# Second block's context attention: one VectorE pass per query chunk takes the maximum over both key halves, for two of four heads

## The reference, cut to what matters

```python
q = jnp.einsum('bsc,hcd->bhsd', xn, wq)
k = jnp.einsum('btc,hcd->bhtd', yn, wk)
v = jnp.einsum('btc,hcd->bhtd', yn, wv)
a = jax.nn.softmax(jnp.einsum('bhsd,bhtd->bhst', q, k) * D ** (-0.5), axis=-1)
o = jnp.einsum('bhst,bhtd->bhsd', a, v)
```

## Time and profile before

| | |
|---|---|
| median of 3 runs | 1450.94 us |
| lowest, highest | 1449.52, 1451.96 us |
| profiled execution, first to last instruction (span) | 1480.6 us |
| profiled execution, own time beside the span | not given |
| mean granted TensorE clock | 0.975 of 2.4 GHz |
| busy: TensorE, VectorE, ScalarE, GpSimd | 1407.8, 837.4, 762.4, 576.4 us |

### The profile page before, as it was taken

How to read it: one execution, slowest core, us unless ns; L and a number is a source line. 1 busy time by engine, 2 the same in 40 slices (tenths; PEclk the granted TensorE clock), 3 DMA queues, 4 the chain that set the end, 5 groups by cost and what they waited for, 6 DMA issues and landing times.

```text
span 1480.6 us, 24805 instructions
## 1 busy us (share of the span) xinstructions
PE 1407.8 (95%) x9880; PEld 807.5 (55%) x9880; DVE 837.4 (57%) x1739; ACT 762.4 (51%) x1161; POOL 576.4 (39%) x629
## 2 busy tenths in 40 slices
PE   8999999999999988899999999998999999997997
PEld 5677853333333256787653433753344445667996
DVE  3288547669999464126763774346788882222221
ACT  4544225656666645233254777332688885323331
POOL 3053134233334333521021565501688886405111
PEclk9999999999999999899999999997799999998999
DMA  7000000000110048562300002404000001833100
GB/s 226 1 1 1 1 12 1 15 8 16 44 40 19 3 152 297 195 220 68 33 23 0 10 24 79 130 0 135 1 10 16 9 16 38 330 118 102 34 17 10
DMA packets 81810, 90.85 MB, mean 61 GB/s; under 512 B 31969, under 2 KB 65726, under 8 KB 80543
## 3 DMA queue, kind: packets, MB, share of 16 engines
q1 hardware_dynamic: 78782, 83.01, 18.2%
q0 software_dynamic: 2912, 6.26, 1.2%
HBM read 67.92 MB, written 21.48 MB: 60 GB/s over the span
## 4 chain that ended last, share of the span: by engine, by line
PE 85%; DVE 9%; issue 2%; ACT 2%; POOL 1%; another core or an unknown queue 1%; DMA 0%; POOLq 0%; DVEq 0%; ACTq 0%
PE psum L1717 12%; PE psum L1736 10%; PE psum L1675 6%; PE psum L4140 6%; PE psum L736 4%; PE psum L3392 4%; PE psum L3383 4%; PE psum L1933 4%; PE psum L1759 3%; PE psum L4151 3%; PE psum L2863 2%; DVE a_nm L1846 2%; PE psum L2869 2%; PE psum L3361 2%; PE psum L724 2%
## 5 line engine op out<-in xcount | busy, mean ns | idle before, releaser
L1846 DVE TENSOR_REDUCE a_nm<-psum 128x1 f32<-128x512 f32 x302 | 199.6, 686 | 99.8 <-PE psum L1675 97.3
L1846 DVE TENSOR_REDUCE xa_nm<-psum 128x1 f32<-128x512 f32 x256 | 161.8, 683 | 49.6 <-PE psum L1675 44.0
L1771 ACT ACTIVATE xn<-psum 128x1024 f32<-128x1024 f32 (+1 forms) x96 | 86.2, 949 | 52.0 <-PE psum L1717 52.0
L1771 ACT ACTIVATE a_w<-psum 128x1024 f32<-128x1024 f32 x86 | 83.4, 1021 | 17.8 <-PE psum L1717 17.3
L1717 PE MATMUL psum<-a2qT,a2kT 32*128 32x512 f32 x512 | 90.3, 608 | 0.0
L1771 ACT ACTIVATE xa_w<-psum 128x1024 f32<-128x1024 f32 (+2 forms) x96 | 79.7, 885 | 19.6 <-PE psum L1717 19.4
L1675 PE MATMUL psum<-a2kr,a2qr 32*128 32x512 bf16 x256 | 71.5, 408 | 6.4 <-DVE a_nm L1846 5.7
L1707 PE MATMUL psum<-a_mrow,onesb 2*128 2x512 bf16 x384 | 69.2, 392 | 0.3 <-DVE a_mrow L1875 0.2
L1675 PE MATMUL psum<-xa_ckr,xa_cqr 32*128 32x512 bf16 x256 | 65.7, 382 | 1.7 <-POOL xa_ckr L1980 1.0
L1675 PEld LDWEIGHTS psum<-a2kr,a2qr 32*128 32x128 bf16 x256 | 20.8, 92 | 76.0 <-DVE a_nm L1846 49.2
L670 POOL TENSOR_SCALAR pf_kdd<-pf_kdd 128x1024 f32<-128x1024 f32 x8 | 22.2, 2775 | 97.2 <-ACT pf_kdd L841 97.2
(11 more groups left out here) (591 smaller groups left out, 3488.4 us busy)
## 6 DMA issues: line engine op xcount, KB each, us to landing
mo_w<-in_L_ffn_W SPq DMA_DIRECT2D x14, 1024.0 KB
sw_wv<-in_L_ffn_w_v SPq DMA_DIRECT2D x4, 2048.0 KB, 18.9
scratch_a2v<-co_stages SPq DMA_DIRECT2D x16, 256.0 KB
scratch_a2k<-co_stages SPq DMA_DIRECT2D x16, 256.0 KB
a2kT<-scratch_a2k SPq DMA_DIRECT2D x8, 512.0 KB, 7.8
a2v<-scratch_a2v SPq DMA_DIRECT2D x4, 1024.0 KB, 11.7
sw_wp<-in_L_ffn_w_proj SPq DMA_DIRECT2D x4, 1024.0 KB, 19.6
a_raw<-scratch_a_dens SPq DMA_DIRECT2D x56, 64.0 KB, 2.1
```

The source lines that it names most:

```text
L1771: e.activation(self.weights(n, c)[:, 2 * jj:2 * jj + 2, lo:S], ps[:, pr:pr + 2, lo:S], ACT.Exp, scale=self.scale).then_inc(*self.weighed.m ...
L1846: e.tensor_reduce(self.nm[n % 3][:, q, part, h:h + 1], view, AX.X, ALU.max, negate=True).then_inc(*self.max_taken.mark(*i))
```

## The change

Keys of heads 2 and 3 in the first half are replaced, in the rounded keys only, by the difference of first and second half. A maximum item of such a head and half ("excess") is then q(k1 - k2), the amount by which the first score exceeds the second. ScalarE copies it with a rectifier instead of plainly. The item of the second half ("lower") is then handled by one VectorE instruction, `tensor_tensor_reduce`: second half plus rectified difference, which is the larger of the two scores, with the sign turned and the minimum over the row as a second output. So heads 2 and 3 have one VectorE pass for two items, heads 0 and 1 two passes as before. The columns of `nm` that no pass writes are set to 1e30 once, by GpSimd. The order of the items changes to [excess, lower, plain, plain], where the lower one belongs to the excess item of the four before; the differences are kept also in the lead-in (in two tiles that are free there), where they are no longer VectorE's. In the planner the kept item no longer has its own VectorE pass right behind the second maximum. GpSimd's rounding becomes three instructions a group. The first attention of the block (`a1`) goes on as before. Not shown: the constructor's and `keep_maxima`'s new arguments, the memset, and the wait on it.

```diff
     def place(self, step):
+        if self.a.is_excess(step[1]):
+            yield from self.keep(step)
+            return
...
-        self.take(step, self.now + time, self.TAKE)
+        self.take(step, max(self.now + time, self.outstanding.pop(step[1], 0.0)), self.TAKE)
...
-        self.held = step[1], self.scalar
+        if self.a.paired:
+            self.outstanding[self.a.taker(step[1])] = self.scalar
+        else:
+            self.held = step[1], self.scalar
...
     def pair_kept(self, n):
 
-        if self.fits(n, "rows"):
+        if self.a.paired:
+            step = self.among(n, self.a.is_excess) or self.among(n, self.is_upper)
+            if step:
+                yield from self.place(step)
+        elif self.fits(n, "rows"):
             yield from self.keep(self.chosen((2, 3)))
 
+    def among(self, n, kind):
+
+        return next((step for step in self.maxima_left()[:4] if kind(step[1])), None) if self.fits(n, "rows") else None
+
+    def is_upper(self, item):
+        return item[3] > 1 and (item in self.outstanding if self.a.is_lower(item) else not self.a.is_excess(item))
+
     def behind_rows(self, n, c):
-        if self.held and self.fits(n, "rows"):
+        if self.a.paired:
+            step = self.among(n, self.is_upper)
+            if step:
+                yield from self.place(step)
+        elif self.held and self.fits(n, "rows"):
             yield from self.place(self.chosen((2, 3)))
         yield from self.held_taken()
 
     def pair_behind(self, n):
         for count in range(2):
-            if self.fits(n, "rows"):
+            if self.a.paired:
+                step = self.among(n, lambda item: item[3] < 2)
+                if step:
+                    yield from self.place(step)
+            elif self.fits(n, "rows"):
                 yield from self.place(self.chosen((0, 1)))
...
+    def paired_items(self, n, t):
+
+        i, half = divmod(t, 2)
+        excess, plain = [(n, i, 0, 2 + half)], [(n, i, half, 0), (n, i, half, 1)]
+        lower = [(n, i, 1, 2) if half else (n, i - 1, 1, 3)]
+        return (excess if t < 2 * SC else []) + (lower if t else []) + (plain if t < 2 * SC else [])
...
-            yield step
+            if step[0] == "max" and self.is_excess(step[1]):
+                self.keep_next(step[1])
+                yield "keep", step[1]
+            else:
+                yield step
...
-                e.activation(kept[:, :], ps[:, self.pair_of("max", *i), :], ACT.Copy).then_inc(*self.max_kept.mark(*i))
+                e.activation(kept[:, :], ps[:, self.pair_of("max", *i), :], ACT.Relu if self.paired else ACT.Copy).then_inc(*self.max_kept.mark(*i))
...
+                elif self.is_lower(i):
+                    w.wait_ge(*self.max_kept.at(*self.excess_of(i)))
+                    kept, _ = self.kept_at(self.excess_of(i))
+                    e.tensor_tensor_reduce(out=kept[:, :], in0=view, in1=kept[:, :], scale=-1.0, scalar=-NEG, op0=ALU.add, op1=ALU.min,
+                                           accum_out=self.nm[n % 3][:, q, part, h:h + 1]).then_inc(*self.max_taken.mark(*i))
...
-            e.tensor_copy(self.kr[b][:, g, :], self.kT[:, g, b * keys:(b + 1) * keys]).then_inc(*self.rounded.mark(b, g))
+            kr, first, early, late = self.kr[b][:, g, :], 32 * self.attention.paired[0], slice(b * keys, b * keys + S), slice(b * keys + S, (b + 1) * keys)
+            e.tensor_copy(kr[:, S:keys], self.kT[:, g, late]).then_inc(*self.rounded.mark(b, g, "late"))
+            w.wait_ge(*self.k.pool.now())
+            e.tensor_copy(kr[0:first, 0:S], self.kT[0:first, g, early]).then_inc(*self.rounded.mark(b, g, "early"))
+            w.wait_ge(*self.k.pool.now())
+            e.tensor_tensor(kr[first:P, 0:S], self.kT[first:P, g, early], self.kT[first:P, g, late], ALU.subtract).then_inc(*self.rounded.mark(b, g))
```

More of the change, by code:

```diff
@@ L1045, in __init__ @@
         self.ahead = 3 if self.folded else 2
-        self.held = None
+        self.held, self.outstanding = None, {attention.taker(item): 0.0 for item in attention.kept_items if ("max", attention.taker(item)) in self.left}
+        attention.early = len(attention.kept_items)
     def begin(self, mode, groups=range(4), after=0.0):
@@ L1284, in __init__ @@
     def __init__(self, k, tag, owner, jobs, d, scale, mem, upper=False, causal=False, weights=(), outs=(), group=1):
-        self.group, self.folded, self.kept = group, d < 32, []
+        self.group, self.folded, self.kept, self.paired = group, d < 32, [], ()
         self.k, self.tag, self.owner, self.jobs, self.d, self.scale, self.upper = k, tag, owner, jobs, d, scale, upper
@@ L1327, in kept_at, with is_excess, is_lower, taker @@
         i = self.kept_items.index(item)
-        return self.kept[i % 2], self.kept_items[i - 2] if i > 1 else None
+        tiles = self.kept_early if i < self.early else self.kept
+        return tiles[i % 2], self.taker(self.kept_items[i - 2]) if i > 1 else None
+    def is_excess(self, item):
+        return item[3] in self.paired and item[2] == 0 and self.jobs[item[0]].mode == "full"
+    def is_lower(self, item):
+        return item[3] in self.paired and item[2] == 1 and self.jobs[item[0]].mode == "full"
+    def taker(self, item):
+        n, i, part, h = item
+        return (n, i, 1, h) if self.paired else item
+    def excess_of(self, item):
+        n, i, part, h = item
+        return n, i, 0, h
     def keep_outs(self, outs):
@@ L1358, in items @@
             return [(n, i, j, 0) for i in range(SC) for j in range(i + 1)]
+        if len(self.paired) == 2:
+            return [item for t in range(2 * SC + 1) for item in self.paired_items(n, t)]
         return [(n, i, half, h) for i in range(SC) for half in range(self.halves(n)) for h in (2, 0, 3, 1)]
+    def paired_items(self, n, t):
[3 more added lines that the diff above has]
+        return (excess if t < 2 * SC else []) + (lower if t else []) + (plain if t < 2 * SC else [])
     def maxima(self):
@@ L1543, in pool_set @@
             e.memset(t[:, :, :, :], -NEG).then_inc(*self.set.mark("parts"))
+        for t in self.nm if self.paired else ():
+            w.wait_ge(*pool.now())
+            e.memset(t[:, :, :, :], -NEG).then_inc(*self.set.mark("halves"))
         for t in self.small if self.folded else ():
@@ L1839, in vector_steps @@
                     w.wait_ge(*(self.max_taken.at(n - 3, "all") if self.folded else self.max_parts.at(n - 3, 1)))
+                if self.paired:
+                    w.wait_ge(*self.set.at("halves"))
                 view = ps[:, self.pair_of("max", *i), :]
@@ L3422, in scalar_program @@
                 e.activation(self.v[:, i, :], ps[:, banks.of(self.pre + "_v", i), :], ACT.Copy).then_inc(*self.value_copied.mark(self.pre, i))
+            else:
+                self.attention.scalar_steps(e, w, [(step, i)])
         self.attention.scalar_steps(e, w, self.attention.order())
```

7 lines of the change are left out of this document (5 added, 2 removed).

## The result

The changed kernel takes 1460.44 us, median of 20 runs, against 1451.45 for the kernel before on the same chip: a ratio of 1.0049 (95% interval 1.0035 to 1.0063), so **about 7 us slower** (5.1 to 9.1; the medians alone are 9.0 apart). The profiled execution has a span of 1458.7 us, against 1480.6. What is compared is durations inside the stage.

A forecast was written before the change was run, and what follows sets the result against it. TensorE was taken as the only full engine, with the second maximum's VectorE pass on the path. Loop 7 jobs x (0.47 - 0.43 + 0.6) = +4.5 us plus lead-in +3.4 gave +7.9, 1458.8 us; range 1444 to 1468.

The forecast's parts named there:

- (1): Context-attention loop: dropping the kept copy's VectorE pass gives back only waits its queue caused, some 0.43 us a job.
- (2): Loop: the combined VectorE pass costs +0.1 us in six of eight steps, +0.6 us a job; bounds 0 and 0.17.
- (3): Loop: the planner moves the maximum rows' transposes to the next job's start, their copy no longer hidden, +0.47 us a job.
- (4): Lead-in: maxima wait for banks behind ScalarE's copies, +2.1, low clock +0.8, a later stall +0.5; +3.4 us, between 0 and 5.
- The second stall: Lead-in, maxima 24 to 26: a maximum needs the bank of a difference behind two query copies on ScalarE, +0.5 us.
- the clock holds: Rival: the lead-in's clock stays at 1.0 in the changed kernel, net some -6.5 us, 1444 us; chance 7%.
- (5): GpSimd forms the keys in three instructions, some 5 us more for four groups, covered by idle time.
- VectorE was the bound: Rival: loop steps start when VectorE's last reductions end, so the change is faster, -8.7 us, 1442 us; chance 12%.
- half rate: Rival: the combined pass streams at half rate, 4 us a job, 28 + 3.4 us, 1482 us; chance 5%.
- the tables: Rival: ScalarE's rectifier needs another table than the exponential, loads twice a step, over 100 us; chance 1%.
- Nothing to see: Rival: combined pass free or hidden by the exact scores, lead-in stall half hidden, 1450 to 1453 us; chance 20%.

The follow-up runs named there:

- batch 3: Third set of timing runs, on its own chip: the kernel before beside four others, among them the changed kernel unchanged again, ratio 1.0053.
- batch 1: First set of timing runs, on its own chip, kernels timed beside the kernel before; the changed kernel, unchanged, had ratio 1.0022.
- a_reduce: Changed kernel with a plain maximum instead of the combined pass, the difference not added; at equal clock its time is the changed kernel's within the interval.
- b0: Kernel before, unchanged, profiled once more; its lead-in was 7.8 us apart from that of its first profile.
- b_round: Kernel before with only GpSimd's rounding of the keys as in the changed kernel, three instructions a group; no effect, lead-in 44.69 us.

## Why the prediction was right, point by point

The time was forecast at 1458.8 us, +7.9; measured were +7.1 and, in batch 3, +7.3 in the mean. The sign and the size hold in these two comparisons; on the chip of batch 1 the changed kernel's mean is only 3.2 us above, within noise. **The size is right by two errors that cancel, and by the luck of the chip**: the loop was put at +4.5 and is +1.2 from its third step on, and the lead-in, put at +3.4, with the first steps behind it is the rest, some 6 us where the clock answers. The split is measured in batch 3 alone (2.6 at equal clock, 4.7 by the clock); for the first comparison the clocks of the kernel before are not on record.

(1) What comes back in the loop, 0.43 a job: right. 0.21 behind the merge and 0.12 + 0.11 in the two steps beside ScalarE's accumulator copies, 0.44 in all. That the kept pass was not on the path is right too.

(2) The combined pass, +0.1 in six of eight steps: **wrong**; this is the term that failed. Its low bound, nothing, was the true value. The reading that the small second instruction would show behind the pass took VectorE's small operations with their whole latency as model, though the text itself noted that such operations overlap. Three steps are longer by 0.07, 0.02 and 0.02, 0.11 a job instead of 0.6, and a_reduce has these without the pass, so they belong to the new order of the maxima; in the first of them the wait is for ScalarE's difference.

(3) The transposes: right, from the planner's numbers alone; +0.43 against +0.47, confirmed from both sides. Over seven jobs it is 3.0 us, all that (1) gives back, where the whole change costs 2.6 at equal clock.

(4) The lead-in: the mechanism right, both sizes off. The stall was put at 2.1 and is 1.25 (3.93 against 2.68), since ScalarE reaches the turn's copies 0.2 us behind the first maximum, not 1.07 as before (b0: 1016.69 and 1017.76). The second stall was put at 0.5; it is 0.34 at half clock (1.13 against 0.79) and 0.56 at full clock. And the low clock was put at 0.8, because the profile had the kernel before at half clock anyway. It is 4.7 on batch 3's chip (0.0048 x 989). The rival that the clock holds was given a place in the changed kernel; it is the *kernel before* in which it often holds (17 of 35 runs of batch 3), so the change had more to lose.

(5) GpSimd: right. 0.61 + 0.61 + 1.27 us a group where 0.5 + 0.5 + 1.28 were put, and covered; b_round shows nothing of it.

Of the rivals, that VectorE was the bound is out: it lost 4.1 us a job, and no step of a steady job is below 2.97. That of half rate is out with the 692 ns, and that of the tables with ScalarE's 21.02 us a job, before 21.03. "Nothing to see" had the combined pass right, and the lead-in's stall nearly (1.25 of the 2.1 us are left); it left out the clock behind it.

## What to carry to other kernels

Taking work off an engine that is not the bound gives only the waits that its queue caused, and a planner that reads its clock will re-place other steps: print the order before and after, and look for what has moved behind its cover. A stall of 1 or 2 us on TensorE ahead of a stretch where the granted clock is in doubt can cost over 4 us more in clock, as it did on one of the three chips of the batches; and whether a kernel's clock holds there can't be read from one profile, but from the granted clocks of many runs. Compare small changes at equal clock, and then ask what they do to the clock.

## What the runs showed of the hardware

- A maximum of a sum, with its accumulator read out, costs VectorE no more than a plain maximum over the same 128x512 in PSUM: 692 ns, and the read's 83 ns end with them, within 0.01 us.
- GpSimd takes as long for 64 partitions as for 128: the casts of 64x512 and 128x512 are 0.61 us each, and the sum of 64x512 takes 1.27 us like the one of 128x512 (1.28).

```profile
937.16 0.61 POOL L3313 CAST a2kr<-a2kT 128x512 bf16<-128x512 f32 x1
937.83 0.61 POOL L3315 CAST a2kr<-a2kT 64x512 bf16<-64x512 f32 x1
938.52 1.26 POOL L3317 TENSOR_TENSOR a2kr<-a2kT 64x512 bf16<-64x512 f32 x1
```

- The same program had its lead-in at a granted clock of 0.94 in one execution and 0.75 in another, 7.8 us apart. Chips differ too: the mean granted clock of the kernel before, over the whole program, was 0.981, 0.980 and 0.986 in the three batches.
